# Experts' output bias: from a TensorE matmul of ones to a VectorE add in the copy out of PSUM

## The reference

```python
sh = gelu(einsum('nd,sdh->snh', xf, sw1) + sb1[:, None, :])
shared_out = (einsum('snh,shd->nd', sh, sw2) + sb2.sum(0)) / S      # S = 2 shared experts
gates = xf @ router_w + router_b
topv, topi = top_k(gates, 2); probs = softmax(topv)
h = gelu(einsum('nd,edh->enh', xf, w1) + b1[:, None, :])            # E = 8 routed experts, 512 hidden
y = einsum('enh,ehd->end', h, w2) + b2[:, None, :]
moe_out = einsum('ne,end->nd', comb, y)                             # comb: the two probabilities of a token
```

## Time and profile before

| | us |
|---|---|
| median of 3 runs (lowest, highest) | 1222.02 (1220.18, 1222.48) |
| the profiled execution, its own time | 1218.74 |
| its span, first to last instruction | 1217.1 |
| PE busy in the span | 1117.4 |
| DVE busy | 885.1 |
| ACT busy | 702.3 |
| POOL busy | 420.2 |

### The profile page before, as it was taken

One profiled execution on the slowest core, in us unless ns is written; L12 is line 12 of the kernel. 1 busy time (PEld: TensorE's weight loads), 2 busy tenths in 40 slices (PEclk: granted clock), 3 DMA queues, 4 the chain that ended last, 5 costly groups with the idle time before them and its releaser, 6 DMA issues. The chain is left out here.

```text
span 1217.1 us, 28139 instructions
## 1 busy us (share of the span) xinstructions
PE 1117.4 (92%) x9260; PEld 946.3 (78%) x9261; DVE 885.1 (73%) x2032; ACT 702.3 (58%) x1585; POOL 420.2 (35%) x559
## 2 busy tenths in 40 slices
PE   4869997999998899999998889879999999998997
PEld 1336665888887677777776489869999999998997
DVE  5858996766676788888888377467766776764666
ACT  1378995556572566667666543346755555554543
POOL 1237895531212011111120026663222232223664
PEclk9879999999998899999999878889999999999999
DMA  9246651000005455354453047656455555544664
GB/s 320 79 167 237 226 193 54 1 0 0 0 0 113 98 119 116 87 108 107 89 107 56 2 169 266 219 203 239 166 167 169 165 161 166 164 139 157 190 206 150
DMA packets 97574, 163.51 MB, mean 134 GB/s; under 512 B 12048, under 2 KB 72228, under 8 KB 95172
## 3 DMA queue, kind: packets, MB, share of 16 engines
q1 hardware_dynamic: 87652, 135.05, 38.1%
q0 software_dynamic: 9104, 26.49, 6.2%
q10 hardware_dynamic: 720, 0.71, 0.2%
HBM read 102.47 MB, written 33.69 MB: 112 GB/s over the span
## 5 line engine op out<-in xcount | busy, mean ns | idle before, releaser
L1796 DVE TENSOR_REDUCE c_mx<-d_bank 128x2 f32<-128x512 f32 x256 | 164.4, 686 | 16.5 <-PE d_bank L1948 16.1
L1711 ACT ACTIVATE c_probs<-c_t 128x512 f32<-128x512 f32 x248 | 134.7, 598 | 26.8 <-PE c_t L1974 25.9
L2929 ACT ACTIVATE d_g_full<-d_bank,d_e_bias 128x256 f32<-128x256 f32 x156 | 77.8, 498 | 105.3 <-PE d_bank L34 105.3
L32 PE MATMUL d_bank<-de_zt_hi,d_e_hi 128*128 128x256 f32 x312 | 91.0, 292 | 0.1
L34 PE MATMUL d_bank<-d_w_hi,d_g_lo 128*128 x312 | 87.8, 281 | 0.0
L33 PE MATMUL d_bank<-de_zt_lo,d_e_hi 128*128 128x256 f32 x312 | 87.8, 281 | 0.0
L33 PE MATMUL d_bank<-d_w_lo,d_g_hi 128*128 x312 | 87.8, 281 | 0.0
L32 PE MATMUL d_bank<-d_w_hi,d_g_hi 128*128 x312 | 87.8, 281 | 0.0
L34 PE MATMUL d_bank<-de_zt_hi,d_e_lo 128*128 128x256 f32 x312 | 87.3, 280 | 0.0
L3089 POOL DMA_INDIRECT d_w_lo<-d_y_rows,d_pos x64 | 65.4, 1021 | 53.3 <-ACT d_g_hi L3102 20.6
L1644 POOL CAST c_ct_hi<-c_c_raw 128x512 fp32r<-128x512 f32 x15 | 9.2, 610 | 212.3 <-PE c_misc L34 212.3
(11 more groups left out here) (433 smaller groups left out, 3849.0 us busy)
## 6 DMA issues: line engine op xcount, KB each, us to landing
d_e_raw<-in_w SPq DMA_DIRECT2D x39, 514.0 KB, 3.7
a_mb<-a_maxima SPq DMA_DIRECT2D x16, 1024.0 KB, 7.5
d_w_hi<-d_zt_kept SPq DMA_DIRECT2D x26, 512.0 KB
d_y_rows<-de_ys SPq DMA_DIRECT2D x39, 256.0 KB, 2.1
d_z_in<-d_z_rows POOLq DMA_DIRECT2D x37, 256.0 KB, 4.4
c_kt<-c_k_hi SPq DMA_DIRECT2D x64, 128.0 KB, 3.1
c_qt<-c_q_hi SPq DMA_DIRECT2D x64, 128.0 KB, 3.8
d_zt_kept<-d_w_hi SPq DMA_DIRECT2D x20, 256.0 KB
```

The lines of the kernel that those rows point to most:

```text
L32: tensor.matmul(out, lhs_hi, rhs_hi, start=start, stop=False)
L1711: act.activation(probs[h % PR][:], t_bank(n, p, k), ACT.Exp).then_inc(exp_done, 1)
L1796: dve.tensor_reduce(mx[n % 2][:, :, k, p:p + 1], s_ps[h % SB], AX.X, ALU.max).then_inc(max_done, 1)
L2929: act.activation(g_full[:, m, :], hid[m][:, 0:TOK], ACT.Gelu, bias=bias[u][:, m:m + 1]).then_inc(gelu_full, 1)
```

## The change

- The preparation of the bias in `moe_route` goes: POOL's clearing of `b_raw2` and `ones`, SP's two loads of `b2_in`, ACT's rounding, DVE's small operations, `own_tiles` with its six instructions, `own_dve` with DVE's wait for the scatter.
- SP loads all ten rows of `b2_in` to each of the 128 partitions (`out_bias`, 10 KB a partition, 1280 KB in all) in one DMA, where the three loads ahead of the pipeline stood.
- POOL, behind its first load of tokens (of tile 2), waits for it, adds the two shared rows, halves them, and adds them to the eight routed rows: nine additions and one multiplication of 128x256 (`share_bias`).
- PE's two bias matmuls a tile and its wait for `own_done` go, DVE's `pick_bias` too.
- DVE's copy out of PSUM becomes an addition of `out_bias[e]`; behind its wait for the tile's sum it reads the tile's expert into a register. Before tile 0 it waits for `share_bias`.
- The second shared expert's weights share one buffer: the first is loaded in step 2, split during tiles 36 and 37, and the second is loaded after that; the load of the first kept chunk moves to step 2 as well.

```diff
@@ moe_route
-        pool.memset(b_raw2[:], 0.0).then_inc(pool_ready, 1)
-        pool.memset(M.ones[:], 1.0)
-        sync.wait_ge(pool_ready, 1)
-        for at in (0, S.BIAS_LO):
-            sync.dma_start(b_raw2[at:at + NE, :], b2_in).then_inc(bias_loaded, 16)
-        act.wait_ge(bias_loaded, 32)
-        act.activation(M.bias2[:], b_raw2[:], ACT.Copy).then_inc(act_ready, 1)
-            if h == 13:
-                own_tiles()
-            if h == 14:
-                for half in range(2):
-                    dve.wait_ge(scattered[half], 16 * TILES * TOP // 2)
-                own_experts(dve)
...
@@ moe_experts
+    out_bias = one("out_bias", [P, S.NE, D])
+    last_raw = one("last_raw", [P, KD * FF])
@@ on_sync
+            if isinstance(i, int) and i == AHEAD:
+                sync.dma_start(s1_raw, w1_in[S.NE - 1, :, 0:KD * FF]...).then_inc(last_loaded, 16)
+                load_kept(0)
+            if isinstance(i, int) and i == LAST_TILE - 2:
+                sync.wait_ge(last_lo, 1)
+                sync.dma_start(s2_raw, w2_in[S.NE - 1]).then_inc(last_loaded, 16)
             sync.wait_ge(y_copied, i + 1)
...
-        sync.dma_start(s1_raw[:], ...).then_inc(last_loaded, 16)
-        sync.dma_start(s2_raw[:], w2_in[S.NE - 1]).then_inc(last_loaded, 16)
-        load_kept(0)
+        sync.dma_start(out_bias[:], b2_in.rearrange("e d -> (e d)").partition_broadcast(P)...).then_inc(bias_loaded, 16)
@@ on_gpsimd, load
             pool.dma_start(z[u][:], z_rows[...]).then_inc(z_loaded[u], 16)
+            if isinstance(i, int) and i == AHEAD:
+                share_bias()
+        def share_bias():
+            shared = out_bias[:, E, :]
+            pool.wait_ge(bias_loaded, 16)
+            for e in range(E + 1, S.NE):
+                pool.tensor_tensor(shared, shared, out_bias[:, e, :], ALU.add).then_inc(bias_shared, 1)
+                pool.wait_ge(bias_shared, e - E)
+            pool.tensor_scalar(shared, shared, 1.0 / (S.NE - E), None, ALU.mult).then_inc(bias_shared, 1)
+            pool.wait_ge(bias_shared, S.NE - E)
+            for e in range(E):
+                pool.tensor_tensor(out_bias[:, e, :], out_bias[:, e, :], shared, ALU.add).then_inc(bias_shared, 1)
@@ on_scalar, first
+            if isinstance(i, int) and i == LAST_TILE - 1:
+                act.wait_ge(last_loaded, 16)
+                act.activation(M.s1_hi[:], s1_raw, ACT.Copy).then_inc(last_hi, 1)
@@ on_vector, second
-            if isinstance(i, int) and i == LAST_TILE - 1:
+            if isinstance(i, int) and i == LAST_TILE - 2:
                 split_last(0, M.s1_lo, s1_raw, M.s1_hi)
             dve.wait_ge(y_done, i + 1)
             after(dve, stored[u], before_last(i, u))
-            dve.tensor_copy(ys[u][:], y_ps[u]).then_inc(y_copied, 1)
+            if isinstance(i, int) and i == 0:
+                dve.wait_ge(bias_shared, S.NE)
+            e = dve.value_load(M.tiles_at[:, 0, bass.ds(i, 1)], min_val=0, max_val=E - 1)
+            dve.tensor_tensor(ys[u][:], y_ps[u], out_bias[:, bass.ds(e, 1), :].broadcast_to([P, T, D]), ALU.add).then_inc(y_copied, 1)
-                pick_bias(dve, i + 2, u)
@@ on_tensor, second
-            pe.wait_ge(own_done, i + 1)
+            pe.wait_ge(gelu_lo, KF * (i + 1))
             for t in range(T):
-                pe.matmul(y_ps[u][:, t, :], own[u][:], M.bias2[:], start=True, stop=False)
-                if t == 0:
-                    pe.wait_ge(gelu_lo, KF * (i + 1))
```

More of the change, by code:

```diff
@@ L2168, in phase_moe @@
             e_loaded = [sem(f"e_loaded{u}") for u in range(2)]
-        route = moe_route(nc, S, M, ctx, sem, x_all, tanh_g, ident, half_neg, routed, w1_in, router_b, b1_in, w2_in, b2_in, z_rows, zt_kept)
-        experts = moe_experts(nc, S, M, ctx, sem, route, ident, passed, w1_in, w2_in, z_rows, y_rows, zt_kept)
+        route = moe_route(nc, S, M, ctx, sem, x_all, tanh_g, ident, half_neg, routed, w1_in, router_b, b1_in, w2_in, z_rows, zt_kept)
+        experts = moe_experts(nc, S, M, ctx, sem, route, ident, passed, w1_in, w2_in, b2_in, z_rows, y_rows, zt_kept)
         combine = moe_combine(nc, S, M, sem, route, experts, x_all, tanh_g, zt_kept, y_rows, out)
@@ L2194, in _ @@
         def _(dve):
-            route.vector(dve, experts.turn_dve, experts.own_dve)
+            route.vector(dve, experts.turn_dve)
             experts.vector(dve)
@@ L2312, in on_sync @@
         sync.dma_start(w2_raw, w2_in[E]).then_inc(shared_loaded, 16)
-        sync.wait_ge(pool_ready, 1)
-        for at in (0, S.BIAS_LO):
-            sync.dma_start(b_raw2[at:at + NE, :], b2_in).then_inc(bias_loaded, 16)
         def load_expert(group):
             if group == 0:
-                sync.wait_ge(ready, 5)
+                sync.wait_ge(ready, 3)
             for e in LOADED[group]:
@@ L2466, in on_scalar, with on_vector @@
         split(3)
-    def on_vector(dve, turn_experts, own_experts):
+    def on_vector(dve, turn_experts):
         def sums(q, some):
@@ L2578, in write_tables @@
             dve.tensor_copy(M.tiles_at[:], tab[:]).then_inc(tables_done, 1)
[L2580 to L2589, removed]
         def split(e):
@@ L2601, in prepare_biases @@
             dve.memset(zero1[:], 0.0).then_inc(ready, 1)
[L2602 to L2610, removed]
+            dve.wait_ge(pool_ready, 2)
         for done in (stats_done, mv_done, z_done):
@@ L2737, in output @@
                 if n == 0:
-                    pe.wait_ge(ready, 5)
+                    pe.wait_ge(ready, 3)
                 if n == MID:
@@ L2793, in moe_route, with moe_experts @@
     return stage
-def moe_experts(nc, S, M, ctx, sem_of, route, ident, passed, w1_in, w2_in, z_rows, y_rows, zt_kept):
+def moe_experts(nc, S, M, ctx, sem_of, route, ident, passed, w1_in, w2_in, b2_in, z_rows, y_rows, zt_kept):
     E, KD, KF, FF, D, T, TOK = S.E, S.KD, S.KF, S.FF, S.D, S.T, S.TOK
@@ L2811, in moe_experts @@
     zt_hi, zt_lo = sb("zt_hi", [P, KD, TOK], F32R), sb("zt_lo", [P, KD, TOK], F32R)
-    own, ys = sb("own", [S.BIAS_ROWS, P], F32R), sb("ys", [P, T, D])
-    s1_raw, s2_raw = one("s1_raw", [P, KD, FF]), one("s2_raw", [P, KF, D])
+    ys = sb("ys", [P, T, D])
+    out_bias = one("out_bias", [P, S.NE, D])
+    last_raw = one("last_raw", [P, KD * FF])
+    s1_raw, s2_raw = last_raw[:].rearrange("p (c f) -> p c f", c=KD), last_raw[:].rearrange("p (m d) -> p m d", m=KF)
     first_kept = one("first_kept", [P, 2 * KD * TOK], F32R)
@@ L2859, in turn_pe @@
         mm.then_inc(zt_done, 1)
[L2861 to L2867, removed]
     def on_sync(sync):
@@ L2968, in split_last @@
             dve.wait_ge(last_hi, k + 1)
-            dve.tensor_tensor(low[:], raw[:], high[:], ALU.subtract).then_inc(last_lo, 1)
+            dve.tensor_tensor(low[:], raw, high[:], ALU.subtract).then_inc(last_lo, 1)
         def second(i, u):
-            if isinstance(i, int) and i == LAST_TILE - 1:
+            if isinstance(i, int) and i == LAST_TILE - 2:
                 split_last(0, M.s1_lo, s1_raw, M.s1_hi)
@@ L3029, in moe_experts @@
     stage.sync, stage.gpsimd, stage.scalar, stage.vector, stage.tensor = on_sync, on_gpsimd, on_scalar, on_vector, on_tensor
-    stage.turn_act, stage.turn_dve, stage.turn_pe, stage.own_dve = turn_act, turn_dve, turn_pe, own_dve
+    stage.turn_act, stage.turn_dve, stage.turn_pe = turn_act, turn_dve, turn_pe
     stage.kept_at, stage.kept_loaded, stage.stored, stage.last_lo = kept_at, kept_loaded, stored, last_lo
```

31 lines of the change are left out of this document (10 added, 21 removed).

## The result

In the first measurement the changed kernel took 1218.41 us in the median of 12 runs (1215.66 to 1221.93), the kernel before 1221.97 us in the median of 12 (1216.59 to 1224.64), the three of the table above among them. The ratio is 0.9974, with 0.9962 to 0.9987 as its 95% interval: 3.2 us are gained, between 1.6 and 4.6. The interval excludes no change, and its middle lies a little over the 0.2% that I had set as what can be told from it. 8.9 us were forecast, so well over half of the gain is missing. That the median lies inside the range, by 0.1 us at its upper end, says little: the range reached that far for stalls of up to 5.9 us, not for what was forecast.

A forecast was written before the change was run, and what follows sets the result against it. The number of PE's instructions in the experts' loop was taken as the bound. Bias matmuls -9.4 us and start stall +0.5 gave -8.9, so 1213.1 us against the median of 1222.02; range 1210.8 to 1218.5.

The forecast's parts named there:

- What bounds the kernel: Experts' loop: bound by the number of PE's instructions alone, 6.373 us a step; what is taken from PE comes off.
- Change 1: Experts' loop on PE: 78 bias matmuls go at 0.120 us each, 9.4 us off, all on the path.
- Change 2: Experts' loop on DVE: register read of 0.8 us and addition instead of copy, covered by idle time, cost nothing.
- Change 3, the start: Start of the experts' stage: bias load and POOL's joining delay PE's tile 2, 0.5 us lost once, ends 0 and 8.3.
- The rule, POOL's end less 861.5: Start of the experts' stage: PE's stall ahead of tile 2 equals POOL's finishing time less 861.5; 0.5 us for 862.0.
- The landing: Broadcast load of all bias rows, issued at 848.29: lands at 854.0 at best, 858.7 at worst; 854.0 taken.
- The multiplication: POOL's one multiplication in joining bias rows: 0.35 us, a quarter of the rounding of 128x1024 in 1.32 us.
- The additions: POOL's nine additions in joining bias rows: 0.85 us each, above the median of 0.77 since DVE works beside it.
- slower: Start: late load and slow additions free POOL at 874.6, PE stalls 13.1 us, clock may halve; 1229 us, chance 0.06.
- Change 4: Route stage's removed instructions and the moved splits and loads of the last weights: all zero, 1 us each if uncovered.
- POOL's additions are drawn out by DVE: Start: POOL stands still during DVE's low parts, free at 864.6, PE stalls 3.1 us; 1215.7 us, chance 0.25.
- The loop does not get shorter: Experts' loop: slow register read or late weights keep the step at 6.37 us, time about 1222; chance 0.07.

The follow-up runs named there:

- the fourth measurement: Profiles on one chip: kernel before 1223.21 us, changed kernel twice 1216.36 and 1216.13, the early join with DVE's register read ahead of its wait 1210.25.
- the third measurement: Timing on a chip that runs both kernels 3% faster: changed kernel unchanged 1180.63 us, kernel before 1183.45, ratio 0.9972; two variants timed beside them.
- the early join: Changed kernel with bias rows loaded in the route stage and joined by POOL before its first load of tokens: 1212.21 us, ratio 0.9951 against the kernel before.
- two POOL instructions: Changed kernel without POOL's eight additions to the experts' rows, so the output lacks the shared bias: 1177.43 us, ratio 0.9949 against the kernel before.

## Why the prediction was wrong

**What bounds the kernel** was right. The loop is PE's alone, what is taken from PE there comes off (8.3 us by the beat with nothing else changed), and nothing in it became a new bound.

**Change 1** was right in kind, a little high: 78 x 0.107 = 8.3 us, not 78 x 0.120 = 9.4. My check spread the whole step evenly over 50 matmuls, so it could not find that the bias matmul is the cheaper one. Its own distance to the matmul after it, 0.11 us in the timeline of before both times in tile 0 (862.74 to 862.85, 864.28 to 864.39), is a hint, though some other distances read 0.11 too. 1.1 us of the error.

**Change 2**, nothing in the loop, was right: the addition takes 0.69 us like the copy, and DVE still waits 1.6 us for PE ahead of it. What I left out is the last tile, behind which no idle time of DVE comes that could hide the register read. The time from the last transposes to the last addition is 14.6 us with the read behind the wait, and 14.0 with the read ahead of it (1084.5 to 1099.1, and 1082.1 to 1096.1 in the fourth measurement). 0.6 us.

**Change 3, the start, is the step that failed.** I took a stall of 0.5 us, with POOL free at 862.0. 1.8 us were measured in two executions and 2.8 to 3.0 in three. The rule, POOL's end less 861.5, has the right form: 863.87 gives 2.4 us against 1.8, and 865.3 gives 3.8 against 3.0; of that surplus 0.3 and 0.6 us are there only because the experts' stage began that much later in these executions than in the profile of before. The terms in it were too small, one by one:

- The landing: 854.0 forecast; 848.5 + 5.9 = 854.4 in the first profile, 849.4 + 6.7 = 856.1 in the fourth measurement. I had the range, 854.0 to 858.7, and took its lower end, because three loads of more bytes had left that place as early. The row of the same kind of load, spoke for more, and was the nearer one.
- The multiplication: 0.35 forecast, 0.88 measured, also where DVE is mostly idle, and 1.72 in the fourth measurement. I had scaled a rounding of 128x1024 down by its columns. POOL's instructions don't scale so: here a multiplication of 256 columns takes 0.88 us and a rounding of 1024 takes 1.05.
- The additions: 9 x 0.85 = 7.65 forecast, 1.38 + 6.89 = 8.27 measured.
- The clock: the fall to half behind a stall stood only in the rival "slower", for stalls of over ten us. Here it came behind waits of 2.3 to 2.8 us. 1.5 us where it happens; no term of the sum had it.

In an execution of the long kind that is the whole error: -8.9 + 1.1 + 0.6 + 2.4 + 1.5 = -3.3, against the 3.2 us timed.

**Change 4** was right, zero. Route took 136.8 to 140.9 us in three profiles of before and 137.4 to 139.4 in four of after, those of the third measurement aside; the splits of the last weights and their loads cost PE no wait.

**The rivals.** "POOL's additions are drawn out by DVE" was the nearer case: it had POOL free at 864.6 and a stall of 3.1 us, against 863.2 to 865.3 and 1.8 to 3.0 measured. In part that is luck: between 854 and 862 it counted one of DVE's low parts of 1.2 us, and the trace of before has two (853.92 and 855.96); with both its stall would have been 4.3 us. It asked for 1215.7 us; the lower price of the matmul, the last tile and the clock fall, 1.1 + 0.6 + 1.5 = 3.2 us, stand against the 2.7 us on to 1218.4. That the two engines hold each other up is seen on both. The eight additions have a median of 0.912 us in after and 0.738 in the early join, where DVE has less to do beside them (and one of 1.73 where it works); in the third measurement, where DVE works beside most of them, those of the early join have 0.909. On DVE, by the groups of lines between 853 and 866 us (times, busy us, mean ns), first of after, then of the early join, where POOL adds nothing in that stretch:

```profile
L2928 DVE TENSOR_TENSOR d_g_lo<-d_g_full,d_g_hi 128x256 fp32r<-128x256 f32 x5 | 4.3, 902 | 0.3 <-ACT d_g_hi L2898 0.3
```
```profile
L2932 DVE TENSOR_TENSOR d_g_lo<-d_g_full,d_g_hi 128x256 fp32r<-128x256 f32 x8 | 3.2, 422 | 1.2 <-ACT d_g_hi L2902 1.2
```

DVE's low parts took 902 ns beside POOL's additions and 422 without them. The same shape twice, and the time more than doubled. In the third measurement, with one edit between the kernels, they took 816 ns on average in after between 838.8 and 845.3 us, and 424 with two POOL instructions. Not all are drawn out: DVE's low parts of 128x1024 took 1.22 us in both of these profiles, and it was POOL's additions beside them that took longer (1.38 and 1.12 us). The Trainium skill, "SBUF — State Buffer", section "Who interferes with whom", has GpSimd and VectorE share one pair of ports, with VectorE's instructions taking part that have two inputs in SBUF; these rows agree, as both inputs of the low parts are there. The rows show that each engine is slower beside the other; that it is the ports is the page's account. I gave that rival 0.25 because at least half of the 60 additions shown in the earlier trace rows were quick; but I had not looked at what DVE did beside them.

"The loop does not get shorter" and "slower" did not come.

## What to carry to other kernels

What is saved a step in a loop is lost again in part when the preparation that makes it possible delays the first steps: put one-time preparation where its engine is idle anyway (here between the last scatter and the first load of tokens), and put a register read ahead of the wait, not behind it. Price a new instruction by a row of its own engine and kind with its fixed part, not by columns alone; and where POOL and DVE work side by side on SBUF, price their instructions drawn out. Read the granted clock behind each stall of PE: in the experts' stage six waits of 2.3 to 3.1 us each had 3.4 us at half clock behind them, and the two of 1.6 had not. And read an idle time against the schedule without it: one of 0.5 us here cost nothing.

## What was unexpected of the hardware

- A multiplication of a 128x256 tile by a constant on POOL takes 0.88 us, longer than the addition of two such tiles, 0.73.
- One bias matmul of 128x256 among others costs 0.107 us, while the average of the step is 0.120. Why is not shown.
- The chips differ by stage and not evenly: after took 114.9, 260.5 and 95.4 us in the third measurement, and 139.0, 253.3 and 115.0 in the first. The loop has the same beat of 6.16 us; the stages around it are shorter by 24 and 20 us. The traces say where: in route PE was idle for 6.0 us and not 19.4, at a mean granted clock of 0.91 and not 0.85; in combine for 5.2 and not 15.5, at 0.99 and not 0.93. DMA moved 269 GB/s in route and not 228. What makes it so was not tried.
